# One 256-column accumulation in place of two of 128 for the sum of squares, with weights stored plain and doubled

## The chip, the core and the metric

The kernel runs on one core of one Trainium2 chip. Time is device microseconds (us) of that core, from launch to end; lower is better. The engines of the core are TensorE (PE; PEld is its weight load), VectorE (DVE), ScalarE (ACT), GpSimd (POOL) and SyncE (SP, which here only issues transfers). Each runs its own list of instructions in order, and they meet at semaphores.

## What is computed

A transformer block with adaptive layer norm on x of 4 x 1024 x 256: attention with 16 heads of 16, then a feed-forward part that picks one of 8 experts for each group of tokens by the smallest reconstruction loss. The part that matters here is the loss:

```python
h = relu(einsum('btd,ndh->bnth', x, W_enc) + b_enc)        # 8 experts, 64 hidden each
recon = einsum('nbth,nhd->nbtd', h, W_dec) + b_dec
losses = mean((recon - x) ** 2, axis=(2, 3))
top1 = argmin(losses, axis=0)
...
return base + adapter_out                                   # adapter of the chosen expert
```

The kernel doesn't form recon. The square of recon summed over the tokens is a sum over pairs of hidden units: (the sum over tokens of h_i h_j) times (W_dec W_dec^T)_ij. The first factor is a product of the hidden values with themselves on TensorE, the second is a table of weights, `ww`, computed once.

## The kernel before, in words

One list of steps, `S.list`, is worked out in Python by `order()`; every engine walks the same list and emits its part of each step, so the order on each engine is fixed when the program is built. A batch (b = 0 to 3) has 64 "units" of attention work: the E steps (scores, exponentiated by ACT into `P`), the PV steps (product with V into `pO`) and the M steps (scores whose row maximum DVE takes, line 1298). Between them `plan()` places the steps of the other stages: layer norm of the next batch (`ln1s` statistics on DVE, `ln1n` normalization on POOL at line 1662, `ln1turn` transposition on PE at line 907), `qk`, `v`, `proj`, and the feed-forward steps of the batch before (`enc`, `ehi`, `half`, `gsq`, `pick`, `select`, `fetch`, `mid`, `out`). After the last unit comes a tail, written out by hand, that ends with the second half of batch 3: `gsq` and `half`, `pick`, `select`, `fetch`, `mid`, `out`.

The banks of the PSUM are shared out in turn among all of these (`pM`, `pE`, `pX`; a step waits until the former user has emptied its bank).

The sum of squares is the step `gsq(b, i, th)`: batch b, pair i of the four groups of 128 hidden units, half th of the tokens, so 4 x 2 x 2 = 16 steps. The hidden values are held as two parts, high and low (`Hs[..., 0, :]` and `Hs[..., 1, :]`). For each group p PE multiplies the high part by both parts side by side, which leaves 256 columns in the bank: 128 of high times high, 128 of high times low. The second counts twice, since low times high is the same by symmetry. DVE then multiplies each 128 columns by `ww[:, p, :]` and adds them up (`tensor_tensor_reduce`, line 1491): with scale 1 for the first block and 2 for the second, into `acc[:, th, 1, p]` and `acc[:, th, 2, p]`. Each such reduction is two rows in a profile: the pass over the columns (CUSTOM_DVE_ANT_0) and the reading of the accumulator. It waits for the one before it (`link`), and the last of a step sets the bank free. The step `half(b, p, th)` does the same once over 258 columns with the table `wd` (line 1469). `pick` sums `acc` over its slots (line 1552).

The table is filled by the step `setupc` near the start (line 1633, DVE): 128 columns for each of 4 groups. `wsplit` (c = 0, 1) is a pair of steps on POOL that splits the encoder weights into high and low parts, `weh` and `wel` (lines 1750 and 1752); it becomes due at unit 24. The pair stands in POOL's list between the steps `ln1s(1, 1)` and `ln1n(1, 1)`.

SP issues all transfers in the order of the list: the moves of the operands `QO` and `KO` (line 1880), the maxima (`QO<-mT`, line 1938), the output of attention (`outs<-osb`, line 1891), the tiles of x for the next layer norm (`xin<-in_x`, line 1948), which wait for the transposition of the tile before. POOL issues 12 transfers of its own at the start (line 1700).

Of the kernel before, what the change touches and what calls it, by code (L numbers as in the profile page):

```python
# [11 lines left out]
ALU = mybir.AluOpType  # L12
# [537 lines left out]
def adaln_block(nc, x, wqkvT, wpT, pb, wbase, bbase, wenc, benc, bencc, wdec, wdecT, bdecT,  # L550
                wdown, bdown, wup, bup, cidx, cT, wmod, consts, out):
    ctx = ExitStack()
    with ctx:
        def sb(name, shape, dt=F):
            return ctx.enter_context(nc.sbuf_tensor(name, shape, dt))

        def sem(name):
            return ctx.enter_context(nc.semaphore(name))
# [34 lines left out]
        weh = sb("weh", [128, 2, 512], R)  # L593
        wel = sb("wel", [128, 2, 512], R)
        wd = sb("wd", [128, 4, D + 2])
        ww = sb("ww", [128, 4, 128])
        wdn = sb("wdn", [128, 2, H])
        wdh = sb("wdh", [128, 2, H], R)
        wdl = sb("wdl", [128, 2, H], R)
# [7 lines left out]
        modT2 = sb("modT2", [128, 4, NB])  # L607
        wdc = sb("wdc", [128, 4])
        sbc = sb("sbc", [128, 4])
# [13 lines left out]
        rec = sb("rec", [128, 4, 4])  # L623
        junk = sb("junk", [128, 258])
        junkx = sb("junkx", [128, 512])
        acc = sb("acc", [128, 2, 3, 4])
        ps = sb("ps", [128, 4])
        pl8 = sb("pl8", [128, 4, 2])
        pl8a = sb("pl8a", [128, 4, 2])
# [59 lines left out]
        s_Hh, s_Hl, s_HL, s_Xh, s_Xl = (sem(n) for n in ("Hh", "Hl", "HLd", "Xh", "Xl"))  # L689

        s_fill, s_rs1, s_xn, s_mhl, s_rs2, s_X = (sem(n) for n in ("fill", "rs1", "xn", "mhl", "rs2", "X"))
        s_modT2, s_sbc, s_wd = (sem(n) for n in ("modT2", "sbc", "wd"))

        s_hh, s_hl, s_hL, s_wen, s_wdn, s_wdL = (
            sem(n) for n in ("hh", "hl", "hL", "wen", "wdn", "wdL"))
# [16 lines left out]
        def bank(s):  # L712
            i = turn[s][0]
            return pM[:, i, :] if i < 3 else pE[:, i - 3, :] if i < 6 else pX[:, :]
# [6 lines left out]
        def full(*s):  # L721
            i, n = turn[s]
            return s_full[i], n + 1

        def emptied(*s):
            i, n = turn[s]
            return s_free[i], n + 1
# [4 lines left out]
        def empties(s):  # L732
            return s_free[turn[s][0]], 1
# [529 lines left out]
        def vector(e):  # L1263
            dve = Waits(e)
            link = Link(s_vlink)
# [22 lines left out]
            for s in S.list:  # L1288
                s, piece = step(s)
# [50 lines left out]
                elif kind == "be":  # L1340
# [4 lines left out]
                    for p in range(4):  # L1345
                        a = e.tensor_scalar(be[:, p, 2 * p:2 * p + 2], bmask, bec[:, p:p + 1], None, ALU.mult)
                    a.then_inc(s_be, 1)

                elif kind == "ln1s":
# [11 lines left out]
                    for t in range(2):  # L1361
                        a = e.bn_aggr(mv1[:, k, t, :], st1[:, k, t, :])
                    a.then_inc(s_mv1, 1)

                elif kind == "ln1n" and s[1] == 0:
# [3 lines left out]
                    for t in range(2):  # L1369
                        a = e.tensor_scalar(xt[:, t, :], xt[:, t, :], mv1[:, k, t, 0:1], rs1[:, k, 1, t:t + 1],  # L1370
                                            ALU.subtract, ALU.mult)
# [25 lines left out]
                elif kind == "ln2s":  # L1397
                    b, k = s[1:]
                    dve.wait_ge(*link.now())
                    for t in (2 * k, 2 * k + 1):  # L1400
                        a = e.bn_aggr(mv2[:, t, :], st2[:, t, :])
                    a.then_inc(s_mv2, 1)

                elif kind == "ln2n" and s[1] == LAST:
# [6 lines left out]
                    for t in (2 * k, 2 * k + 1):  # L1411
                        a = e.tensor_scalar(Xr[:, t % 4, :], x2[:, t, :], mv2[:, t, 0:1], rs2[:, 1, t:t + 1],
                                            ALU.subtract, ALU.mult)
# [50 lines left out]
                elif kind == "half" and last:  # L1464
                    b, p, th = s[1:]
# [7 lines left out]
                elif kind == "gsq":  # L1473
                    b, i, th = s[1:]
                    if (b, i, th) == (LAST, 0, 1):
# [5 lines left out]
                        e.tensor_tensor(pl8a[:, :, :], ps[:, :].unsqueeze(2).to_broadcast([128, 4, 2]),  # L1481
                                        bmask.unsqueeze(1).to_broadcast([128, 4, 2]), ALU.mult).then_inc(s_pick, 1)
                        dve.wait_ge(s_pick, 2 * b + 2)
                    dve.wait_ge(*full("setupc"))
                    dve.wait_ge(*full(*s))
                    for p in (2 * i, 2 * i + 1):

                        for r in range(2):
                            dve.wait_ge(*link.now())
                            n = 256 * (p % 2) + 128 * r  # L1490
                            a = e.tensor_tensor_reduce(junk[:, 0:128], bank(s)[:, n:n + 128], ww[:, p, :], r + 1.0, 0.0,
                                                       ALU.mult, ALU.add, acc[:, th, 1 + r, p:p + 1])
                            a.then_inc(*(empties(s) if p % 2 and r else link.up()))
                    dve.wait_ge(*emptied(*s))

                elif kind == "xhi" and alone(s[1], s[2] // 2):
# [141 lines left out]
        def gpsimd(e):  # L1638
# [8 lines left out]
            for s in S.list:  # L1647
# [98 lines left out]

                elif kind == "wsplit":
                    c = s[1]
                    pool.wait_ge(d_w[6], 16)
                    e.tensor_copy(weh[:, c, :], wenc_s[:, c, :]).then_inc(*link.up())  # L1750
                    pool.wait_ge(*link.now())
# [288 lines left out]
```

## Time and profile before

| | us |
|---|---|
| median of 3 runs | 980.05 |
| lowest and highest of them | 978.15, 981.6 |
| the profiled execution, its own time | 980.53 |
| span of the profile, from first to last instruction | 978.7 |
| busy: PE, DVE, ACT, POOL | 945.7, 793.5, 657.7, 335.8 |
| granted TensorE clock, mean | 0.983 |

The span is 1.8 us less than the profiled execution's own time (980.53 - 978.7); that part lies outside the instructions. Busy time is the union of an engine's rows. PE is busy for 97% of the span, DVE for 81%; TensorE's clock is granted at 0.98 of its full 2.4 GHz on the mean. Where a row says "[0.32 <-POOL xin L1662]", the engine stood idle for 0.32 us before it, and the write of `xin` on POOL at line 1662 ended that wait.

### The profile page before, as it was taken

What the parts mean: (1) busy time and instruction counts of PE and PEld (TensorE: products, weight loads), DVE (VectorE), ACT (ScalarE), POOL (GpSimd) and SP (SyncE); (2) the same over time, 40 slices, a digit from 0 to 9 for tenths busy, and PEclk for the clock granted to TensorE, in tenths of its full rate; (3) what the DMA queues carried; (4) which work ended last, traced back from release to release, by engine and by line L of the source; (5) the groups of instructions that cost most, each with busy time, mean ns of one, the idle gap of its engine ahead of it and who ended that gap; (6) DMA issues with size and microseconds to landing.
All of it is one profiled execution on the core that took longest, in us unless ns stands there. A gap on an engine that the chain in (4) does not pass through costs nothing.

```text
span 978.7 us, 16476 instructions
## 1 busy us (share of the span) xinstructions
PE 945.7 (97%) x5794; PEld 475.7 (49%) x5794; DVE 793.5 (81%) x1629; ACT 657.7 (67%) x1295; POOL 335.8 (34%) x447
## 2 busy tenths in 40 slices
PE   6999999989999999999999999999999999999998
PEld 4444344434344355544454455445445465644486
DVE  4789988978888787887788888778878888888365
ACT  2148887877786777666668786766657867566930
POOL 4050234124364343111456543410165613116320
PEclk9889999999999899999999999999999999999999
DMA  6932061342525311416342411405434321132001
GB/s 180 144 73 39 23 110 46 61 93 73 94 49 89 60 36 35 77 27 110 99 105 50 87 35 46 75 14 88 127 82 83 52 36 36 39 98 79 30 6 49
DMA packets 47890, 66.93 MB, mean 68 GB/s; under 512 B 12139, under 2 KB 32112, under 8 KB 47796
## 3 DMA queue, kind: packets, MB, share of 16 engines
q1 hardware_dynamic: 46572, 65.00, 31.4%
q0 software_dynamic: 384, 0.79, 0.6%
q8 instruction: 46, 0.75, 0.4%
q14 instruction: 36, 0.29, 0.1%
q10 hardware_dynamic: 852, 0.09, 0.1%
HBM read 27.48 MB, written 12.59 MB: 41 GB/s over the span
## 4 chain that ended last, share of the span: by engine, by line
PE 75%; DVE 10%; DMA 5%; SPq 4%; ACT 2%; issue 2%; POOL 2%; ACTq 0%; DVEq 0%; POOLq 0%
PE pE L813 23%; PE pM L813 22%; PE pO L813 20%; PE pX L813 8%; DVE mx L1298 7%; SPq L1880 2%; DMA QO<-lo 1%; DMA xin<-in_x 1%; DMA QO<-mT 1%; ACT P L1120 1%; DMA outs<-osb 1%; PE pM L907 1%; ACT h1T L1161 1%; DVE junk L1435 1%; SPq L1938 1%
## 5 line engine op out<-in xcount | busy, mean ns | idle before, releaser
L1298 DVE TENSOR_REDUCE mx<-pE 128x1 f32<-128x512 f32 x440 | 287.2, 683 | 48.7 <-PE pE L813 47.4
L1298 DVE TENSOR_REDUCE mx<-pM 128x1 f32<-128x512 f32 x447 | 294.4, 683 | 31.2 <-PE pM L813 29.6
L1120 ACT ACTIVATE P<-pM 128x512 f32<-128x512 f32 x457 | 260.9, 602 | 69.2 <-PE pM L813 67.7
L1120 ACT ACTIVATE P<-pE 128x512 f32<-128x512 f32 x431 | 243.3, 602 | 86.9 <-PE pE L813 85.8
L813 PE MATMUL pO<-P,V 128*17 128x512 f32 x2048 | 261.7, 607 | 1.2 <-ACT osb L1127 1.0
L813 PE MATMUL pM<-KO,QO 48*128 48x512 f32 x447 | 178.7, 446 | 4.1 <-DMA QO<-lo 3.6
L813 PE MATMUL pM<-QO,KO 50*128 50x512 f32 x457 | 178.6, 435 | 1.0
L813 PE MATMUL pE<-KO,QO 48*128 48x512 f32 x440 | 175.0, 447 | 3.3 <-DVE mx L1298 2.5
L813 PE MATMUL pE<-QO,KO 50*128 50x512 f32 x431 | 166.2, 437 | 3.5 <-DMA QO<-mT 3.0
L813 PEld LDWEIGHTS pM<-QO,KO 50*128 50x128 f32 x457 | 80.8, 187 | 101.4 <-issue 70.8
L813 PEld LDWEIGHTS pE<-QO,KO 50*128 50x128 f32 x431 | 76.0, 187 | 99.4 <-issue 75.7
L1298 DVE TENSOR_REDUCE mx<-pX 128x1 f32<-128x512 f32 x137 | 93.7, 684 | 16.9 <-PE pX L813 16.2
L1120 ACT ACTIVATE P<-pX 128x512 f32<-128x512 f32 x136 | 81.3, 598 | 21.8 <-PE pX L813 21.4
L813 PEld LDWEIGHTS pO<-P,V 128*17 128x17 f32 x2048 | 40.9, 96 | 102.1 <-issue 92.2
L813 PEld LDWEIGHTS pM<-KO,QO 48*128 48x128 f32 x447 | 78.3, 188 | 17.1 <-issue 6.8
L813 PEld LDWEIGHTS pE<-KO,QO 48*128 48x128 f32 x440 | 75.9, 187 | 16.3 <-DVE mx L1298 7.0
L1706 POOL CAST mh<-mxc 128x16 fp32r<-128x16 f32 x32 | 6.3, 198 | 175.5 <-DVE mxc L1307 175.4
L813 PE MATMUL pX<-KO,QO 48*128 48x512 f32 x137 | 62.0, 453 | 2.5 <-DMA QO<-lo 1.1
L813 PE MATMUL pX<-QO,KO 50*128 50x512 f32 x136 | 58.9, 433 | 1.3 <-DVE mx L1298 1.1
L1765 POOL TENSOR_TENSOR Hs<-h2f,Hs 128x512 fp32r<-128x512 f32 x28 | 35.7, 1282 | 67.1 <-ACT Hs L1240 52.9
L1692 POOL CAST hi<-lo 128x512 fp32r<-128x512 f32 x28 | 17.3, 619 | 73.6 <-ACT lo L1180 73.6
L813 PEld LDWEIGHTS pX<-QO,KO 50*128 50x128 f32 x136 | 25.6, 188 | 26.9 <-issue 18.5
(303 smaller groups left out, 1323.0 us busy)
## 6 DMA issues: line engine op xcount, KB each, us to landing
outs<-osb SPq DMA_DIRECT2D x31, 256.0 KB, 2.2
KO<-hi SPq DMA_DIRECT2D x56, 128.0 KB, 4.0
QO<-hi SPq DMA_DIRECT2D x56, 128.0 KB, 5.6
x<-in_x SPq DMA_DIRECT2D x20, 256.0 KB, 3.5
out<-x SPq DMA_DIRECT2D x16, 256.0 KB, 2.1
AT<-outs SPq DMA_DIRECT2D x15, 256.0 KB
asum<-wsum SPq DMA_DIRECT2D x15, 256.0 KB
KO<-lo SPq DMA_DIRECT2D x28, 128.0 KB, 3.7
```

What stands on the lines that cost most here:

```text
L813: return e.matmul(o, lhsT, rhs, start=start, stop=stop)
L907: a = e.transpose(o[:, 256 * c + 128 * t:256 * c + 128 * t + 128], tokens(b, k)[:, t, 128 * c:128 * c + 128], ident)
L1120: e.activation(P[:, u % 3, j, :], bank(s), ACT.Exp).then_inc(*empties(s))
L1161: a = e.activation(h1T[:, c, 256 * k:256 * k + 256], bank(s)[:, 256 * c:256 * c + 256], ACT.Identity, bias=modT[:, c, b:b + 1], scale=modT ...
L1298: e.tensor_reduce(mx[:, hq % 2, k:k + 1, kh], bank(s), AX.X, ALU.max, negate=True).then_inc(*empties(s))
L1435: e.tensor_tensor_reduce(junk[:, 0:D], wd[:, p, 0:D], bc[:, 1, :], 1.0, 0.0, ALU.mult, ALU.add, sbc[:, p:p + 1]).then_inc(*link.up())
L1692: e.tensor_copy(hi[:, cs], lo[:, cs].bitcast(F)).then_inc(s_qh, 1)
L1706: e.tensor_copy(mh[:, :], mxc[:, :]).then_inc(*link.up())
L1765: e.tensor_tensor(Hs[:, t % 4, :, 1, :], h2f[:, t % 2, :].rearrange("p (a n) -> p a n", a=4), Hs[:, t % 4, :, 0, :].bitcast(F), ALU.subtra ...
L1880: e.dma_start(*move(gi, w, i, thirds(gi, w))).then_inc(landed(gi)[0], 16)
L1938: e.dma_start(*rows(hq, j)).then_inc(d_m[hq % 2][j], 16)
```

## The change

`ww` gets 256 columns for each group: the plain weights in columns 0 to 127 as before, and twice the weights in columns 128 to 255. DVE makes one reduction over the 256 columns of a group, with scale 1, where it made two over 128. `acc` loses one of its three slots. The doubled half is written by POOL, in the second `wsplit` step, from the plain half, and `gsq` waits for that (`s_ww`) in place of `setupc`. The memory set aside for the descriptors of POOL's own transfers goes from 4096 to 2048 bytes per partition, which makes room for the larger table.

```diff
-        ww = sb("ww", [128, 4, 128])
+        ww = sb("ww", [128, 4, 256])
...
-        acc = sb("acc", [128, 2, 3, 4])
+        acc = sb("acc", [128, 2, 2, 4])
...
-                    dve.wait_ge(*full("setupc"))
+                    dve.wait_ge(s_ww, 1)
                     dve.wait_ge(*full(*s))
                     for p in (2 * i, 2 * i + 1):
 
-                        for r in range(2):
-                            dve.wait_ge(*link.now())
-                            n = 256 * (p % 2) + 128 * r
-                            a = e.tensor_tensor_reduce(junk[:, 0:128], bank(s)[:, n:n + 128], ww[:, p, :], r + 1.0, 0.0,
-                                                       ALU.mult, ALU.add, acc[:, th, 1 + r, p:p + 1])
-                            a.then_inc(*(empties(s) if p % 2 and r else link.up()))
+                        dve.wait_ge(*link.now())
+                        n = 256 * (p % 2)
+                        a = e.tensor_tensor_reduce(junk[:, 0:256], bank(s)[:, n:n + 256], ww[:, p, :], 1.0, 0.0,
+                                                   ALU.mult, ALU.add, acc[:, th, 1, p:p + 1])
+                        a.then_inc(*(empties(s) if p % 2 else link.up()))
...
                 elif kind == "wsplit":
                     c = s[1]
+                    if c:
+                        pool.wait_ge(*emptied("setupc"))
+                        e.tensor_scalar(ww[:, :, 128:256], ww[:, :, 0:128], 2.0, None, ALU.mult).then_inc(s_ww, 1)
                     pool.wait_ge(d_w[6], 16)
...
-    nc = bacc.Bacc("TRN2", target_bir_lowering=False, num_devices=1, dynamic_dma_scratch_size=4096)
+    nc = bacc.Bacc("TRN2", target_bir_lowering=False, num_devices=1, dynamic_dma_scratch_size=2048)
```

The order on PE, ACT and SP is the same in both kernels. On POOL one instruction is added. POOL before, from the second statistics of the next layer norm to the third (`rs` is the inverse deviation, `xin` the tile that PE transposes, `mh` and `mhl` the maxima in two parts):

```order
L1655 TENSOR_TENSOR rs<-rs,nh 128x2
L1750 CAST weh<-h2f 128x512
L1752 TENSOR_TENSOR wel<-h2f,weh 128x512
L1750 CAST weh<-h2f 128x512
L1752 TENSOR_TENSOR wel<-h2f,weh 128x512
L1662 TENSOR_SCALAR xin<-xin,mv,rs 128x256 x2
L1706 CAST mh<-mxc 128x16
```

The same place on POOL now:

```order
L1654 TENSOR_TENSOR rs<-rs,nh 128x2
L1752 CAST weh<-h2f 128x512
L1754 TENSOR_TENSOR wel<-h2f,weh 128x512
L1750 TENSOR_SCALAR ww<-ww 128x4x128
L1752 CAST weh<-h2f 128x512
L1754 TENSOR_TENSOR wel<-h2f,weh 128x512
L1661 TENSOR_SCALAR xin<-xin,mv,rs 128x256 x2
L1705 CAST mh<-mxc 128x16
```

The doubling stands between the two halves of the weight split, ahead of the normalization of `xin` and of the first conversion of the maxima.

On DVE the reductions of a `gsq` step go from four to two. DVE before in the tail, the last of the two `gsq` steps of the last half batch, then the last `half` and the first two rows of `pick`:

```order
L1491 ISA junk,acc<-pM,ww 128x128
L1491 ISA acc 128x1
L1491 ISA junk,acc<-pM,ww 128x128
L1491 ISA acc 128x1
L1491 ISA junk,acc<-pM,ww 128x128
L1491 ISA acc 128x1
L1491 ISA junk,acc<-pM,ww 128x128
L1491 ISA acc 128x1
L1469 ISA junk,acc<-pE,wd 128x258
L1469 ISA acc 128x1
L1552 TENSOR_REDUCE ps<-acc 128x4
L1554 TENSOR_TENSOR pl<-ps,cst 128x8
```

The same place on DVE now:

```order
L1490 ISA junk,acc<-pM,ww 128x256
L1490 ISA acc 128x1
L1490 ISA junk,acc<-pM,ww 128x256
L1490 ISA acc 128x1
L1469 ISA junk,acc<-pE,wd 128x258
L1469 ISA acc 128x1
L1551 TENSOR_REDUCE ps<-acc 128x4
L1553 TENSOR_TENSOR pl<-ps,cst 128x8
```

Nothing else changes place; two pairs of rows are gone from every `gsq` step, and the remaining ones are twice as wide.

## Rows read from the trace of the kernel before

**Rows 1.** The page: busy time of each engine, its share, instructions.

```profile
PE 945.7 (97%) x5794; PEld 475.7 (49%) x5794; DVE 793.5 (81%) x1629; ACT 657.7 (67%) x1295; POOL 335.8 (34%) x447
```

**Rows 2.** The page: the chain that ended last, by engine.

```profile
PE 75%; DVE 10%; DMA 5%; SPq 4%; ACT 2%; issue 2%; POOL 2%; ACTq 0%; DVEq 0%; POOLq 0%
```

**Rows 3.** Instructions of line 1491 and who waited for them; ns minimum/median/maximum.

```profile
L1491 DVE CUSTOM_DVE_ANT_0 junk<-pE,ww x32: 281/291/294, 406.9 to 950.4; 128x128 f32<-128x128 f32 x32
...
  PEld pX L813: 1.5, 2
  PE pX L813: 0.7, 1
  PEld pE L813: 0.5, 1
```

**Rows 4.** Instructions of line 1469, the reduction over 258 columns.

```profile
L1469 DVE CUSTOM_DVE_ANT_0 junk<-pM,wd x11: 417/427/428, 351.0 to 944.8; 128x258 f32<-128x258 f32 x11
```

**Rows 5.** Timeline of DVE near the end: start us, us, engine, line, instruction.

```profile
944.34 0.43 DVE L1469 CUSTOM_DVE_ANT_0 junk<-pX,wd 128x258 f32<-128x258 f32 x1
...
944.81 0.43 DVE L1469 CUSTOM_DVE_ANT_0 junk<-pM,wd 128x258 f32<-128x258 f32 x1
...
948.04 0.28 DVE L1491 CUSTOM_DVE_ANT_0 junk<-pE,ww 128x128 f32<-128x128 f32 x1
...
950.70 0.69 DVE L1459 TENSOR_TENSOR h2f<-pX,nbe 128x512 f32<-128x512 f32 x1
```

**Rows 6.** Timeline of PE, 649 to 650 us.

```profile
649.63 0.50 PE L813 MATMUL pX<-KO,QO 48*128 48x512 f32 x1 [0.70 <-DVE acc L1491]
```

**Rows 7.** Timeline, the two other places where PE waits for line 1491.

```profile
344.98 0.18 PEld L813 LDWEIGHTS pX<-KO,QO 48*128 48x128 f32 x1 [0.49 <-DVE acc L1491]
...
572.83 0.18 PEld L813 LDWEIGHTS pE<-KO,QO 48*128 48x128 f32 x1 [0.50 <-DVE acc L1491]
...
573.90 0.34 PEld L813 LDWEIGHTS pO<-P,V 128*17 128x17 f32 x8 [0.51 <-ACT P L1120]
```

**Rows 8.** Timeline of PE and PEld in the tail, weight loads and products of the last `half`.

```profile
956.32 0.42 PEld L813 LDWEIGHTS pE<-Xs,Hs 128*128 128x128 f32 x3 [0.23 <-DVE Hs L1533]
956.92 1.14 PEld L813 LDWEIGHTS pE<-Xs,Hs 128*128 128x128 f32 x9 [0.18 <-DVE Hs L1533]
...
960.73 1.62 PE L813 MATMUL pE<-Xs,Hs 128*128 128x258 f32 x12
```

**Rows 9.** Timeline of DVE in the tail, the last `half`, right behind `gsq`.

```profile
962.76 0.43 DVE L1469 CUSTOM_DVE_ANT_0 junk<-pE,wd 128x258 f32<-128x258 f32 x1
```

**Rows 10.** Timeline of POOL in and after the second half of the weight split.

```profile
133.58 0.62 POOL L1750 CAST weh<-h2f 128x512 fp32r<-128x512 f32 x1
134.27 1.28 POOL L1752 TENSOR_TENSOR wel<-h2f,weh 128x512 fp32r<-128x512 f32 x1
135.53 2.45 POOL L1662 TENSOR_SCALAR xin<-xin,mv,rs 128x256 f32<-128x256 f32 x2
137.93 0.20 POOL L1706 CAST mh<-mxc 128x16 fp32r<-128x16 f32 x1
```

**Rows 11.** Timeline of PE, the transposition that reads `xin`.

```profile
138.13 0.63 PE L907 MATMUL pE<-cst,xin 128*128 128x128 f32 x4 [0.32 <-POOL xin L1662]
```

**Rows 12.** Groups of POOL: busy us, mean ns of one, idle before.

```profile
L1789 POOL TENSOR_SCALAR rs<-mv 128x2 f32<-128x2 f32 x16 | 3.7, 234 | 22.2 <-DVE mv L1401 22.2
L1811 POOL TENSOR_SCALAR bc<-bc 128x256 f32<-128x256 f32 x4 | 3.4, 862 | 15.7 <-DVE wd L1445 15.7
```

**Rows 13.** Timeline of SP and DVE after that place.

```profile
141.74 0.45 SPq L1948 DMA_DIRECT2D xin<-in_x  x1
...
146.18 0.75 DVE L1359 BATCH_NORM_STATS2 st<-xin 128x6 f32<-128x256 f32 x2 [0.38 <-DMA xin<-in_x]
```

**Rows 14.** Pieces of the chain that ended last, two landings of `QO<-lo`: start, us, what.

```profile
21.02 5.29 DMA QO<-lo
...
250.86 9.16 DMA QO<-lo
```

More of the change, by code:

```diff
@@ L691, in adaln_block @@
         s_fill, s_rs1, s_xn, s_mhl, s_rs2, s_X = (sem(n) for n in ("fill", "rs1", "xn", "mhl", "rs2", "X"))
-        s_modT2, s_sbc, s_wd = (sem(n) for n in ("modT2", "sbc", "wd"))
+        s_modT2, s_sbc, s_wd, s_ww = (sem(n) for n in ("modT2", "sbc", "wd", "ww"))
         s_hh, s_hl, s_hL, s_wen, s_wdn, s_wdL = (
```

## The prediction

> **What bounds the kernel now.** I read the busy shares first, then the chain of work that ended last, then the timeline around each instruction that the change touches. PE is busy for 97% of the span and DVE for 81% [rows 1]; the chain lies 75% on PE and 10% on DVE [rows 2]. So time taken off DVE is worth something only where PE is waiting for DVE, and a delay is worth its full length wherever PE waits for the delayed thing. Busy totals can't decide this change; sixteen `gsq` steps and one spot on POOL can.
>
> Around the 64 reductions of line 1491 the list of those who waited is short: 1.5, 0.7 and 0.5 us in four entries, of which two describe the same wait, once for the weight load and once for the product [rows 3]. It is three places, at 345, 573 and 650 us. In the tail the chain is serial and DVE has its turn twice.
>
> **The change on DVE.** A 128-column pass takes 291 ns [rows 3], and the read of the accumulator comes behind it. The cost of both in a row is the distance of the starts: eight of them fill the time from 948.04 to 950.70, so 2.66 / 8 = 0.333 us each. The new shape doesn't occur, but its neighbour does: 258 columns, one operand in the PSUM and one table in SBUF, 427 ns [rows 4], with 944.81 - 944.34 = 0.47 us from start to start [rows 5]. So a pair costs 2 x 0.333 = 0.67 us before and 0.47 after, 0.195 us less; a step (two pairs) 0.39 us less; all 32 pairs 6.2 us less of DVE's time. That is 0.6% of the span, and an upper bound of the gain.
>
> **What of it reaches the path, in the loop.** Twelve of the sixteen steps lie among the attention units; 12 x 0.39 = 4.7 us is their bound. At 650 us PE waits 0.70 us for the last reduction of a step [rows 6]; that step ends 0.39 earlier, and the step before it hands on about 0.1 more, since DVE doesn't rest between the two: 0.5 us gained. At 345 us the weight load waits 0.49 us; about 0.17 of this is the usual gap between two loads, so 0.3 is left. At 573 us there is the same wait of 0.50, but half a microsecond behind it PE waits 0.51 for ACT, whose work doesn't hang on this step [rows 7]; what is gained is lost there: 0. At the other nine steps DVE comes to rest, or is held by PE, before PE needs it; I give them 0.1 together. Sum 0.9 us; bounds 0.2 (only half of the place at 650) and 4.7 (every step on the path).
>
> **What reaches it in the tail.** The first eight reductions (948.04 to 950.70, [rows 5]) stand ahead of the chain `enc`, `ehi`, `elo` that feeds `half`. They shrink by 0.78 us, and PE's two waits for `Hs`, 0.23 and 0.18 us [rows 8], nearly vanish: PE runs 0.38 us earlier. The last eight shrink by 0.78 too. Before, the last `half` reduction starts on DVE at 962.76, right behind `gsq` [rows 9], while the product that it reads ends at 960.73 + 1.62 = 962.35 [rows 8]. After, `gsq` would be done by 961.6, and the product, 0.38 earlier, ends at 961.97; the reduction starts at about 962.05, 0.7 us earlier. Between it and the last product of `select` PE has small products of its own to do, which moved by only 0.38; so I take 0.6. Everything behind (`select`, `fetch`, `mid`, `out`) hangs on that product and moves with it. Bounds 0.38 and 0.78.
>
> **The change on POOL.** One tensor_scalar of 128 x 512 is added. POOL has no such shape. Of one-operation tensor_scalars it has 2 columns in 234 ns and 256 in 862 ns [rows 12]: 2.47 ns per column, so 512 cost 0.862 + 256 x 0.00247 = 1.5 us. Bounds: 0.6 us, as the conversion of the same size, and 2.46 us, two of the two-operation ones over 256 columns, which take 2.45 [rows 10].
>
> The price of the place is the point. POOL is 34% busy over the span [rows 1], but not here: from 133.58 to 138.1 us its rows follow each other without a gap, conversion, subtraction, normalization of `xin`, maxima [rows 10]. The doubling goes ahead of all of them. The normalization ends at 135.53 + 2.45 = 137.98 and PE's transposition, next in PE's list, starts at 138.13 after a wait of 0.32 us for it [rows 11]. There is no cover at all: PE is already waiting, so the transposition starts 1.5 us later, and the rest of PE's list with it. The maxima (`mh`) are late by as much too, but PE's transposition of them stands behind several more bursts of scores, so they cost nothing. The wait for `setupc` costs nothing either: DVE does that step near the start, far ahead of this place.
>
> Some is given back. The next tile's transfer is issued at 141.74, held by other transfers and not by the transposition, and DVE waits 0.38 us for it at 146.18 [rows 13]. With PE and DVE 1.5 us late the tile is there in time, so 0.38 is absorbed. Further waits for transfers up to 343 us hang on moves released by PE's or DVE's own progress and shift along. Net cost 1.5 - 0.38 = 1.1 us; bounds 0.2 and 2.1.
>
> Here a page bears on the size. The row says 2.47 ns per column, some 3 cycles of a 1.2 GHz engine. The Trainium skill, page "GPSIMD Engine Reference", section 3.1 "Elementwise — side-by-side cycle accounting", says that a loop body of up to two operations goes at 1.03 cycles per element, limited by the port alone. By that 512 elements would take, as an estimate, 0.44 us and the dispatch; no row of a POOL tensor_scalar here is that fast.
>
> The smaller `acc` shortens two tiny sums on DVE by 4 to 8 elements: nothing. The smaller descriptor memory touches only the 12 transfers that POOL issues at the start.
>
> **The sum.** -0.9 (loop) - 0.6 (tail) + 1.1 (POOL) = -0.4 us. Against the profiled execution, 980.53, that is 980.1. That execution is 0.5 above the median of the runs, 980.05, so the forecast for a median is 979.7. A difference under 0.3%, 2.9 us, is about what a measurement of this kernel can't tell from no change.
>
> **Rivals.**
> *All of the gain reaches the path.* Moving DVE forward may let PE run ahead at steps where I see no wait, since each relieved bank also feeds the next burst of scores. For it: DVE is on the chain for 10% [rows 2]. Against it: only three waits name line 1491 [rows 3]. It gives -4.7 - 0.6 + 1.1 = -4.2, so 975.9. Half of it would give 977.9. Chance of being faster by over 2.9: 0.13.
> *The doubling is cheap.* It costs 0.6 us like the conversion [rows 10]; net cost 0.6 - 0.38 = 0.2, sum -1.3, so 978.8. It is the result of the page's rule, and still within 0.3%. Chance 0.12.
> *The doubling is dear.* 2.46 us, 2.1 net, and only 0.2 gained in the loop: +1.3, so 981.3. This one is slower than before, and decides from the point where the doubling costs more than 0.38 + 0.9 + 0.6 = 1.9 us; still within 0.3%. Chance 0.12.
> *A late transfer.* The stall at 138 us moves all of PE's later requests against transfers that are already under way. The same move `QO<-lo` took 5.29 us at one place of the chain and 9.16 at another [rows 14]. One more meeting of this kind costs 9.16 - 5.29 = 3.9 us: -0.4 + 3.9 = +3.5, so 983.6. For it: DMA is 5% of the chain [rows 2]. Against it: PE shifts by only 1.1 us. Chance 0.07.
> *The halved descriptor memory holds POOL up.* Its 12 early transfers would wait for each other, with operands for the first scores behind them. One such landing, at the 5.29 us of the early `QO<-lo` [rows 14], would make +4.9, so 985. Chance 0.04.
> *The wide pass isn't cheaper.* If it took the 0.67 us of two, the gain is zero and the cost stays: +1.1, so 981.2. Against it stand 32 rows of 258 columns at 427 ns [rows 4]. Chance 0.02.
>
> **How the numbers follow.** The forecast, two small effects that nearly cancel, has the other 0.50. The likeliest time is 979.7. Faster by over 0.3%: 0.13. Slower by over 0.3%: 0.07 + 0.04 = 0.11, and 0.01 for the dear doubling together with something else: 0.12. Within: 0.75. The range reaches from the middle of the first rival, with some 0.08 below it, to beyond the dear doubling, with some 0.09 above it: 977.0 to 982.6.
>
> **What would show it.** In the changed profile: line 1490 with 32 passes at 420 to 428 ns and 32 reads; the doubling on POOL at about 133.6 us with 1.5 us; the wait of the transposition for `xin` at 1.8 us in place of 0.32, and the 0.38 us wait of DVE for the next tile gone; the rows up to 131 us unchanged in time; PE at 345 us about 1.1 us later than before; the 0.70 us wait at 650 down to about 0.2; and the last `half` reduction 0.6 to 0.7 us nearer to the end of the preceding `gsq`'s product than now. The prediction is wrong if the shift after 140 us isn't about 1.1 us, or if the distance from 345 us to the tail shrinks by much more than 0.9.

## The result

The changed kernel takes 983.0 us (median of 22 runs, 980.25 to 990.02) against 979.93 us for the kernel before (22 runs beside them, 978.05 to 985.83). The ratio is 1.0034, 95% interval 1.0019 to 1.0049: slower by 0.34%, some 3.1 us. The forecast was 979.7, within 0.3%, with a range up to 982.6. The time lies 0.4 us above the range, and the sign of the difference is not the one forecast.

Nearly every single term of the sum came out as predicted. One term was missing: what the pause before the transposition does to TensorE's clock.

The page after, busy time and chain by engine, which answer to [rows 1, 2]:

```profile
PE 948.2 (97%) x5794; PEld 477.6 (49%) x5794; DVE 787.9 (80%) x1565; ACT 656.9 (67%) x1295; POOL 336.7 (34%) x448
...
PE 78%; DVE 9%; DMA 4%; ACT 3%; SPq 2%; issue 2%; POOL 2%; ACTq 0%; DVEq 0%
```

PE has the same 5794 products and is busy 2.5 us longer (945.7 before). The same work takes longer: this is the first sign that it isn't only a matter of waiting. The profiled execution took 982.64 us, its span is 980.8 (978.7 before) and its mean granted clock 0.979 (0.983 before).

**The reductions.** Line 1490 in the profile after (count, ns minimum/median/maximum, first and last start), and who waited for it (us, times), which answer to [rows 3]:

```profile
L1490 DVE DVE_READ_ACCUMULATOR2_ANT acc<- x32: 81/83/85, 348.8 to 964.1; 128x1 f32 x32
L1490 DVE CUSTOM_DVE_ANT_0 junk<-pE,ww x16: 413/424/427, 411.3 to 952.3; 128x256 f32<-128x256 f32 x16
...
  PEld pX L813: 0.8, 2
  PE pX L813: 0.3, 1
```

A wide pass takes 424 ns. The timeline of DVE in the tail (start us, us, instruction) gives the distance of the starts, and the rows answer to [rows 5, 9]:

```profile
950.91 0.42 DVE L1490 CUSTOM_DVE_ANT_0 junk<-pE,ww 128x256 f32<-128x256 f32 x1
...
952.30 0.42 DVE L1490 CUSTOM_DVE_ANT_0 junk<-pE,ww 128x256 f32<-128x256 f32 x1
...
952.77 0.69 DVE L1459 TENSOR_TENSOR h2f<-pX,nbe 128x512 f32<-128x512 f32 x1
...
964.78 0.43 DVE L1469 CUSTOM_DVE_ANT_0 junk<-pE,wd 128x258 f32<-128x258 f32 x1 [0.55 <-PE pE L813]
```

Four fill 952.77 - 950.91 = 1.86 us, 0.465 each. The last `half` reduction now waits for its product by 0.55 us, where it stood right behind `gsq` before. At 650 us the wait of 0.70 [rows 6] has become 0.30:

```profile
651.73 0.49 PE L813 MATMUL pX<-KO,QO 48*128 48x512 f32 x1 [0.30 <-DVE acc L1490]
```

**The doubling.** The timeline of POOL, PE and DVE after, which answers to [rows 10, 11, 13]:

```profile
133.06 1.52 POOL L1750 TENSOR_SCALAR ww<-ww 128x512 f32<-128x512 f32 x1
...
136.50 2.45 POOL L1661 TENSOR_SCALAR xin<-xin,mv,rs 128x256 f32<-128x256 f32 x2
```

```profile
139.09 0.63 PE L907 MATMUL pE<-cst,xin 128*128 128x128 f32 x4 [1.83 <-POOL xin L1661]
...
141.26 2.00 PE L813 MATMUL pE<-wqkv_s,h1T 128*128 128x256 f32 x4
143.19 0.79 PE L813 MATMUL pE<-QO,KO 50*128 50x512 f32 x1
```

```profile
148.12 0.74 DVE L1359 BATCH_NORM_STATS2 st<-xin 128x6 f32<-128x256 f32 x2
```

It takes 1.52 us, and PE's wait has grown from 0.32 to 1.83, by 1.51. DVE no longer waits for the next tile. All that was predicted. What wasn't stands in the last row of PE: a product of 512 columns takes 0.79 us, where it takes 0.50 at 139.65 in the same profile. Stretches of 4 us show why (columns: stretch, us; busy us and count of PE, PEld, DVE, ACT, POOL; granted clock; share of DMA; GB/s). After:

```profile
137.00:141.00 4.00, 1.95 (x14) 1.07 (x10) 1.58 (x5) 1.58 (x4) 2.48 (x5) 1.00 0.59 102
141.00:145.00 4.00, 4.00 (x15) 2.07 (x19) 2.06 (x4) 2.82 (x7) 0.00 (x0) 0.57 0.47 117
145.00:149.00 4.00, 4.00 (x33) 1.41 (x29) 3.85 (x10) 3.00 (x8) 0.00 (x0) 1.00 0.09 25
...
202.00:206.00 4.00, 3.89 (x16) 1.35 (x18) 1.89 (x3) 1.93 (x4) 0.00 (x0) 0.60 0.20 24
206.00:210.00 4.00, 4.00 (x12) 1.65 (x12) 1.89 (x4) 1.97 (x5) 0.00 (x0) 0.50 0.56 171
210.00:214.00 4.00, 4.00 (x22) 1.03 (x24) 2.54 (x5) 2.23 (x5) 0.00 (x0) 0.62 0.71 225
```

The same stretches before:

```profile
141.00:145.00 4.00, 4.00 (x30) 1.26 (x29) 3.22 (x7) 3.56 (x8) 0.00 (x0) 1.00 0.43 115
...
202.00:206.00 4.00, 4.00 (x18) 1.16 (x10) 2.29 (x4) 2.48 (x5) 0.00 (x0) 0.66 0.19 67
206.00:210.00 4.00, 4.00 (x31) 1.50 (x32) 3.65 (x7) 3.15 (x6) 0.00 (x0) 1.00 0.73 191
210.00:214.00 4.00, 4.00 (x22) 1.60 (x22) 3.82 (x8) 3.15 (x6) 0.58 (x3) 1.00 0.41 141
```

Behind the longer pause PE's clock is granted at half, 1.2 in place of 2.4 GHz, for most of the stretch from 141 to 145 us (0.57 on the mean), and PE does 15 products where it did 30. It is busy throughout, so that nothing in busy shares or waits names the loss. The half clock doesn't begin with the first product behind the pause: the transposition starts at 139.09, and the clock falls at 141.4. Near 200 us PE waits for `QO<-mT` in both kernels, before and after:

```profile
200.17 0.47 PE L813 MATMUL pE<-QO,KO 50*128 50x512 f32 x1 [2.68 <-DMA QO<-mT]
```

```profile
202.11 0.46 PE L813 MATMUL pE<-QO,KO 50*128 50x512 f32 x1 [2.71 <-DMA QO<-mT]
```

The half clock behind that lasts from 201.3 to 204.7 before, and from 202.8 to 213.0 in this profile of after.

**Where the time went in this pair of profiles.** I took the start of the same product on PE in both, and the difference (after minus before):

| place, us | difference | step | what lies there |
|---|---|---|---|
| 137 | -0.54 | -0.54 | differences of the first 137 us |
| 139 | +0.97 | +1.51 | the longer wait for `xin` |
| 143 | +2.50 | +1.53 | half clock behind it |
| 150 | +1.93 | -0.57 | wait for the next tile absorbed |
| 212 | +4.91 | +2.98 | longer half clock after the wait for `QO<-mT` |
| 340 | +4.71 | -0.20 | |
| 346 | +4.41 | -0.30 | `gsq` at 345 |
| 470 | +4.43 | +0.02 | |
| 490 | +2.64 | -1.79 | a half-clock stretch at 481 in before's profile alone |
| 580 | +2.45 | -0.19 | `gsq` at 573 |
| 655 | +2.10 | -0.35 | `gsq` at 650, less than 0.1 of it drift |
| 880 | +1.93 | -0.17 | |
| 940 | +2.87 | +0.94 | a half-clock stretch at 885 in after's profile alone |
| 974 | +2.13 | -0.74 | the tail |

The stretches at 481 and 885 stand in one profile each and behind no change of the order: further profiles, below, have such stretches at 715, 904, 909 or 912 or nowhere. Which of the entries belong to the change, one pair can't tell. That is what the experiments are for.

### The profile page after: what moved, and what is told of

Same layout as the page of the kernel before. It is cut to its first block, busy times and chain, and to the rows that moved or that the text cites. A ratio compares the mean times of both kernels' runs of the same rounds, so it can differ in the third digit from the quotient of the medians.

```text
span 980.8 us, 16414 instructions
## 1 busy us (share of the span) xinstructions
PE 948.2 (97%) x5794; PEld 477.6 (49%) x5794; DVE 787.9 (80%) x1565; ACT 656.9 (67%) x1295; POOL 336.7 (34%) x448
## 4 chain that ended last, share of the span: by engine, by line
PE 78%; DVE 9%; DMA 4%; ACT 3%; SPq 2%; issue 2%; POOL 2%; ACTq 0%; DVEq 0%
PE pE L813 24%; PE pM L813 23%; PE pO L813 21%; PE pX L813 9%; DVE mx L1298 6%; SPq L1882 2%; DMA QO<-lo 1%; ACT P L1120 1%; DMA QO<-mT 1%; ACT h1T L1161 1%; DVE junk L1435 1%; DMA xin<-in_x 1%; PE pM L907 1%; DMA P<-in_wmod 0%; DVE st L1395 0%
## 5 line engine op out<-in xcount | busy, mean ns | idle before, releaser
L813 PE MATMUL pM<-QO,KO 50*128 50x512 f32 x457 | 180.6, 439 | 0.9
```

What stands on the lines that cost most here:

```text
L813: return e.matmul(o, lhsT, rhs, start=start, stop=stop)
```

## The experiments

The theory: the doubling's place costs its length and, behind it, a stretch of half clock on PE that the longer pause brings on; without the half clock the change would be as forecast, about nothing. The rivals: the layout or the halved descriptor memory costs the time; the new order on DVE does; the rest is chance.

Times are compared with runs of the kernel before on the same chip in the same rounds. Their median is 980.97 us beside the doubling near the start, the doubling alone, the layout alone and the four products; 982.0 beside the two products, the doubling behind `xin`, the doubling twice, and the doubling near the start with the pause at 200 us filled; 980.76 beside the last three, the changed kernel once more and it and the kernel before with that pause filled. Times of different groups are compared by their ratios to before. The ratios are those on record, with 95% intervals; they differ from the quotient of the two medians by up to 0.14%.

### The doubling near the start

The changed kernel, but POOL doubles the table right behind DVE's `setupc`, near the start, in place of the second `wsplit`.

```diff
+                elif kind == "setupc":
+                    pool.wait_ge(*emptied(*s))
+                    e.tensor_scalar(ww[:, :, 128:256], ww[:, :, 0:128], 2.0, None, ALU.mult).then_inc(s_ww, 1)
...
                 elif kind == "wsplit":
                     c = s[1]
-                    if c:
-                        pool.wait_ge(*emptied("setupc"))
-                        e.tensor_scalar(ww[:, :, 128:256], ww[:, :, 0:128], 2.0, None, ALU.mult).then_inc(s_ww, 1)
```

> The changed kernel, but POOL doubles the table in the step setupc near the start, where POOL stands idle for 25 us, instead of between the halves of the weight split. Theory A (the loss is PE's pause for xin at 138 us and the half clock that follows it): no pause and no half-clock stretch at 141 us; what is left is the gain of the wide reductions, -0.3 at 345, -0.2 at 573, -0.4 at 650 and -0.75 in the tail, so about -1.5 us, 978.4. Rival B (the loss comes from the wide reductions, the smaller descriptor memory or the moved tables): it stays slower than before by 2 us or more.

Measured: 978.91 us, ratio 0.9973 (0.9953 to 0.9994). One of the 12 executions took 4684 us and is left out of the ratio; the median of the other 11 is 978.71. The kernel is faster than before by 0.27%, and so some 0.6% faster than the changed kernel, by the place of one instruction of 1.5 us. PE's transposition and the products behind it, and the stretch that follows:

```profile
138.66 0.63 PE L907 MATMUL pE<-cst,xin 128*128 128x128 f32 x4 [0.31 <-POOL xin L1661]
...
140.82 1.13 PE L813 MATMUL pE<-wqkv_s,h1T 128*128 128x256 f32 x4
```

```profile
141.00:145.00 4.00, 4.00 (x28) 1.74 (x32) 3.22 (x7) 3.58 (x8) 0.00 (x0) 1.00 0.34 82
```

The wait is 0.31 again, the clock full, and the four products of `wqkv_s` take 1.13 us in place of 2.00. The gains of the wide reductions stay: -0.29 at 345, -0.19 at 573, -0.42 at 650, -0.80 in the tail. What DVE gains is worth its 1.7 us (their sum) once the doubling is out of the way. The wide reductions on DVE are acquitted.

### The doubling alone

The kernel before with narrow reductions, plus the doubling at the changed kernel's place, into a table that nobody reads, and the smaller descriptor memory.

```diff
+        ww2 = sb("ww2", [128, 4, 128])
...
                     c = s[1]
+                    if c:
+                        pool.wait_ge(*emptied("setupc"))
+                        e.tensor_scalar(ww2[:, :, :], ww[:, :, :], 2.0, None, ALU.mult)
...
-    ... dynamic_dma_scratch_size=4096)
+    ... dynamic_dma_scratch_size=2048)
```

> The kernel before with its narrow reductions; a spare table in SBUF, the smaller descriptor memory, and the same doubling on POOL in the second wsplit step, written to the spare table that nobody reads. Theory A: PE pauses 1.5 us longer at 139 us, a stretch at half clock follows and costs about 1.5 more, some 0.5 is absorbed: +2.5 us at least, and more than the changed kernel by the 1.5 us that its reductions save, so +3 to +5. A theory of the pause alone, without the clock: +1.0. Rival B: nothing, within 0.5 us.

Measured: 983.61 us, ratio 1.0021 (0.9997 to 1.0045). The interval just holds 1, so by time alone this is weak; the profile is not:

```profile
139.12 0.63 PE L908 MATMUL pE<-cst,xin 128*128 128x128 f32 x4 [1.82 <-POOL xin L1663]
...
141.28 2.08 PE L814 MATMUL pE<-wqkv_s,h1T 128*128 128x256 f32 x4
```

```profile
141.00:145.00 4.00, 4.00 (x15) 2.17 (x19) 1.98 (x4) 2.75 (x6) 0.00 (x0) 0.57 0.57 134
```

The wait, the half clock, and the shift of PE against before (-0.51 at 137, +0.99 at 139, +2.55 at 143, +1.97 at 150) are those of the changed kernel's first profile within 0.05 us, without a single wide reduction. At 345, 573 and 650 this kernel gains nothing (0.01 each), and in the tail nothing either (+0.01). The time alone doesn't show what was expected further, that this kernel is slower than the changed one by the gain of its reductions: 1.0021 here, 1.0034 there, with intervals wider than that gain.

### The layout alone

The kernel before with the same spare table, never written, and the descriptor memory of 2048 bytes.

```diff
+        ww2 = sb("ww2", [128, 4, 128])
...
-    ... dynamic_dma_scratch_size=4096)
+    ... dynamic_dma_scratch_size=2048)
```

> The kernel before with the smaller descriptor memory and a spare table in SBUF, so that the tensors lie where the changed kernel has them; no instruction differs. Theory A: no difference, within 0.5 us. Rival B in its form of the descriptor memory: slower by 2 us or more.

Measured: 980.59 us, ratio 0.9991 (0.9966 to 1.0017). PE stands where it stood before, within 0.2 us, from 100 to 470 us. Memory and layout are out as a cause.

### PE kept busy in the pause

The changed kernel, and ahead of the transposition's wait PE makes products that nobody uses, the identity by 512 columns of `wqkv_s`, into the bank that the transposition then overwrites. Four of them:

```diff
                     b, k = s[1:]
+                    if (b, k) == (1, 1):
+                        for _ in range(4):
+                            mm(o, ident, wqkv_s[:, 0, 0:512])
                     pe.wait_ge(s_xn if b else s_xn0, nth["ln1n", b, k] - (4 if b else 0))
```

> The changed kernel; ahead of the wait for xin of ln1turn(1, 1) PE makes four products of the identity with 512 columns of wqkv_s into the bank that the transposition overwrites. They fill the pause of 1.8 us, the doubling stays where it is. Theory A: the pause keeps its length but the stretch at half clock after it is gone, so 1.5 us or more faster than the changed kernel, at +1 to +1.5 over before. A theory of the pause alone: no faster than the changed kernel, +3.

Measured: 980.91 us, ratio 1.0004 (0.9985 to 1.0023). Each of these products is two instructions of 0.46 us, so that the four took 3.7 us, twice the pause: PE was 3.91 us late at 139 (with 0.78 at 137) against 0.97 in the changed kernel. Yet the clock stayed full from 141 to 145, and although 2 us had been thrown away, the kernel was no slower than before, and better than the 1 to 1.5 us of loss expected. Behind the wait at 200 us (2.73 here) the half clock lasts from 205.7 to 212.6, twice as long as before, although there was none at 141; PE's shift grows there by 1.4:

```profile
141.00:145.00 4.00, 3.78 (x17) 2.04 (x15) 1.84 (x3) 2.30 (x5) 0.00 (x0) 1.00 0.41 92
...
206.00:210.00 4.00, 4.00 (x14) 1.74 (x12) 1.92 (x4) 2.17 (x4) 0.00 (x0) 0.50 0.45 151
```

The edit was mis-sized; the next one puts it right, with two products:

```diff
-                        for _ in range(4):
+                        for _ in range(2):
```

> As the run that filled the pause, but with two products of the identity with 512 columns in place of four: each turned out to be two instructions of 0.46 us, so four took 3.7 us and held PE 2 us longer than the doubling does; two take 1.85 us, the length of the pause. Theory A (the pause costs 1.5 us, the half clock behind it 1.5 more): clock 1.00 from 141 to 145 us, PE 1.5 to 1.7 us late at 143 us and not 3.0 as in the changed kernel, the whole 1 to 1.5 us faster than the changed kernel, near 981. A theory of the pause alone: PE 3.0 us late at 143 us whatever PE does in the pause.

```profile
137.47 1.98 PE L813 MATMUL pE<-wqkv_s,cst 128*128 128x512 f32 x4
139.29 0.65 PE L910 MATMUL pE<-cst,xin 128*128 128x128 f32 x4
```

```profile
141.00:145.00 4.00, 3.95 (x25) 1.97 (x25) 3.22 (x7) 3.57 (x8) 0.00 (x0) 1.00 0.52 128
```

Measured: 981.5 us, ratio 0.9999 (0.9981 to 1.0017). The transposition starts as late as in the changed kernel (the shift grows by 1.45 there, from -0.27 to 1.18), so the delay is all there, but the clock is 1.00 and the shift goes to 1.17 at 143 and 0.70 at 150. **This is the run that tells most.** With the delay kept and the half clock gone, the change is worth what the prediction said of it, nothing that can be measured (-0.04% forecast, -0.01% measured, interval -0.19 to +0.17%). The delay itself was priced rightly.

### The doubling behind xin

The changed kernel, with the doubling on POOL right behind the normalization of `xin`, ahead of the maxima.

```diff
+                    if (b, k) == (1, 1):
+                        pool.wait_ge(*emptied("setupc"))
+                        e.tensor_scalar(ww[:, :, 128:256], ww[:, :, 0:128], 2.0, None, ALU.mult).then_inc(s_ww, 1)
...
                     c = s[1]
-                    if c:
-                        pool.wait_ge(*emptied("setupc"))
-                        e.tensor_scalar(ww[:, :, 128:256], ww[:, :, 0:128], 2.0, None, ALU.mult).then_inc(s_ww, 1)
```

> The changed kernel, with the doubling on POOL one step later: behind the normalization of xin, ahead of the maxima. Theory A (only what PE waits for costs, and at this place it waits for xin alone): no pause at 138 us, no half clock at 141, as fast as with the doubling near the start, -1.5 to -2.7 us against before. Rival (the place costs because POOL is dense there, whoever is behind it): the maxima are 1.5 us late, PE or SP waits for them, and it is slower than with the doubling near the start by 1 us or more.

```profile
138.27 0.63 PE L907 MATMUL pE<-cst,xin 128*128 128x128 f32 x4 [0.31 <-POOL xin L1661]
```

Measured: 979.68 us, ratio 0.9981 (0.9961 to 1.0001). PE waits 0.31 us for `xin`, the clock stays full, and the shift is 0.15 at 137 and 0.13 at 143. It is 0.59 at 150, as DVE waits 0.83 us for the next tile; with the doubling near the start that wait is 0.72 and the shift grows alike, by 0.35. The maxima are 1.5 us late here and nobody on PE is: the prediction's claim that they have cover holds. So it is the place ahead of `xin` by one instruction of POOL that costs, not the doubling.

### The doubling twice

The doubling alone once more, but done twice, so that the pause is longer by 1.5 us again.

```diff
                         pool.wait_ge(*emptied("setupc"))
+                        e.tensor_scalar(ww2[:, :, :], ww[:, :, :], 2.0, None, ALU.mult).then_inc(*link.up())
+                        pool.wait_ge(*link.now())
                         e.tensor_scalar(ww2[:, :, :], ww[:, :, :], 2.0, None, ALU.mult)
```

> The kernel before with the doubling into a spare table made twice, one behind the other, in the second wsplit step: 3.0 us on POOL. Theory A: PE's pause grows by 3.0 us and the half clock follows once, so PE is 3.0 + 1.5 to 2 us late at 145 us, and the whole is +4.5 to +6 us. If the clock loss grew with the pause, it would be +3.0 in its place and the whole +7 or more. A theory of the pause alone: +2.5.

```profile
140.48 0.63 PE L908 MATMUL pE<-cst,xin 128*128 128x128 f32 x4 [3.37 <-POOL xin L1663]
```

```profile
141.00:145.00 4.00, 4.00 (x13) 2.25 (x12) 1.94 (x3) 2.48 (x5) 0.00 (x0) 0.52 0.52 133
145.00:149.00 4.00, 4.00 (x21) 1.41 (x20) 2.36 (x5) 2.43 (x5) 0.00 (x0) 0.62 0.04 9
```

Measured: 984.85 us, ratio 1.0040 (1.0023 to 1.0057), some 3.9 us, a little under the 4.5 to 6 expected. The shift goes from -0.70 at 137 to 2.35 where the transposition starts (the pause, 3.05) and 4.97 when the half clock is over: it lasts into the next stretch, from 141.2 to 148.0, and costs 2.62 us, where it cost 1.56 in the profile of the single doubling. And the long half clock at 203 us is not there: in this profile it takes 3.4 us as in before, and PE's shift goes from 4.40 at 150 to 4.41 at 212. So that one isn't a fixed consequence of a late PE.

### The changed kernel once more

To see which stretches return, the changed kernel with no edit.

> The changed kernel as it is, on the chip and in the rounds of the next two runs. It should be +2 to +4 us against before, with the same pause at 138 us and the clock at 0.57 from 141 to 145 us. What is asked of it: whether the long stretch at half clock behind the second pause (202.8 to 213 us, in this kernel and in the one with the doubling alone; 3.4 us long in before) comes again.

```profile
140.27 0.83 PE L907 MATMUL pE<-cst,xin 128*128 128x128 f32 x4 [1.83 <-POOL xin L1661]
```

```profile
141.00:145.00 4.00, 4.00 (x13) 2.34 (x12) 1.89 (x3) 2.48 (x5) 0.00 (x0) 0.50 0.39 102
145.00:149.00 4.00, 4.00 (x25) 1.55 (x28) 2.66 (x5) 2.73 (x6) 0.00 (x0) 0.70 0.15 40
...
206.00:210.00 4.00, 4.00 (x16) 1.12 (x8) 2.28 (x5) 2.54 (x5) 0.00 (x0) 0.65 0.19 67
210.00:214.00 4.00, 4.00 (x31) 1.47 (x30) 3.65 (x7) 3.11 (x6) 0.00 (x0) 1.00 0.67 179
```

Measured: 983.02 us, ratio 1.0032 (1.0013 to 1.0051), the same as the first time. The wait of 1.83 us and the half clock behind it come back, this time from 140.6 to 147.4 us: the half clock begins earlier, in the transposition itself (0.83 us in place of 0.63). The shift goes from 0.63 at 137 to 2.15 where the transposition starts (1.52, the pause) and 4.66 when the half clock is over, so that this costs 2.51 us for the same pause that cost 1.53 the first time, and nearly as much as behind the pause of twice the added length. The long one at 203 does not come back (+0.0 from 150 to 212). The half clock behind the doubling's pause is thus in every profile of a kernel that leaves this pause open, and lasts 3.4 us in two of them and 6.8 in three (the third, below, is the changed kernel with another pause filled); that near 200 is common to all that leave that pause open, and its length varies too.

### Filling the pause at 200 us

Every kernel above waits 2.4 to 2.7 us for `QO<-mT` at 200 us and then runs at half clock. Three of the same unused products stand ahead of that wait, 2.8 us, in three kernels: the one with the doubling near the start, the changed one, and the one before.

```diff
                     gi, c = SEQ[hq]
+                    if (u, j) == (48, 0):
+                        for _ in range(3):
+                            mm(o, ident, wqkv_s[:, 0, 0:512])
                     if gi:
                         pe.wait_ge(*landed(gi))
```

With the doubling near the start:

> The kernel with the doubling near the start; in addition PE makes three products of the identity with 512 columns of wqkv_s, 2.8 us, into its own free bank while it waits 2.6 us for QO<-mT at 198 to 201 us (unit 48). Theory A, carried to another pause: the stretch at half clock that now follows at 202 us is gone, which gives 1.0 to 1.7 us, so 977.2 to 977.9. If that stretch isn't due to the pause: no gain, within 0.5 us of the kernel with the doubling near the start.

```profile
198.82 2.84 PE L813 MATMUL pE<-wqkv_s,cst 128*128 128x512 f32 x6
```

```profile
202.00:206.00 4.00, 4.00 (x26) 1.44 (x23) 3.63 (x6) 3.64 (x7) 0.00 (x0) 1.00 0.20 65
```

Measured: 976.11 us, ratio 0.9954 (0.9936 to 0.9972). The clock stays full where it was 0.66 before, and the shift goes from +1.34 at 200.5 us to -0.25 at 212: 1.6 us gained by work that nobody needs. A second half-clock stretch, at 238 us, went too, for reasons that I didn't find. The time is 1.1 us below the 977.2 to 977.9 expected; the shift shows the second stretch to be worth 1.45. The kernel leaves nothing of the computation out, and it is faster than both kernels of this document.

In the changed kernel:

> The changed kernel with the three products in the second pause, at unit 48, and nothing in the first. If the 2.8 us that the changed kernel loses between 201 and 213 us are the clock behind the second pause, they go, and the stretch of before with them: PE between 200 and 213 us gains 3.5 to 4 us on the changed kernel, the whole is 3 to 4 us faster than it, about 979. If the first pause is what makes the second stretch long, and filling the second can't help, it gains 1 us at most.

```profile
141.00:145.00 4.00, 4.00 (x12) 2.38 (x12) 1.89 (x3) 2.57 (x6) 0.00 (x0) 0.50 0.30 76
...
202.00:206.00 4.00, 4.00 (x19) 1.32 (x17) 1.43 (x3) 1.41 (x3) 0.00 (x0) 1.00 0.63 88
```

Measured: 980.3 us, ratio 0.9998 (0.9981 to 1.0015). The pause at 138 is left as it is, with its half clock (0.50 from 141 to 145). At 200 the shift falls from 3.74 to 2.15, again 1.6, and at 238 by 1.45 more. The changed kernel with one pause filled is level with the kernel before.

In the kernel before:

> The kernel before, with narrow reductions, and the same three products in its second pause. It parts the gain of the fill from that of the wide reductions: the stretch at 201 us goes, -1.0 to -1.7 us; the kernel with early doubling and fill stays ahead of it by the 1.5 us of the reductions.

```profile
202.00:206.00 4.00, 4.00 (x24) 1.60 (x23) 3.62 (x6) 3.51 (x7) 0.00 (x0) 1.00 0.22 71
```

Measured: 978.8 us, ratio 0.9973 (0.9959 to 0.9987). The shift goes from 1.04 to -0.43 over the pause, 1.5 gained; the stretch at 237 stayed here. The profile has one more half-clock stretch, at 715 us, that costs it 3.2 us and that no other profile has; the median of the runs is faster than before all the same.

### The clock over all runs

Each run records a mean granted clock. Over the runs of each kernel it is:

| kernel | runs | mean clock | time, us | PE's added pause at 138 |
|---|---|---|---|---|
| before | 88 | 0.9822 | 980 to 982 | none |
| changed | 22 | 0.9784 | 983.0 | 1.51 |
| changed, once more | 12 | 0.9792 | 983.02 | 1.51 |
| doubling alone | 12 | 0.9800 | 983.61 | 1.50 |
| doubling twice | 8 | 0.9797 | 984.85 | 3.05 |
| changed, pause filled (two) | 12 | 0.9826 | 981.5 | filled |
| changed, pause filled (four) | 12 | 0.9842 | 980.91 | filled |
| doubling behind `xin` | 12 | 0.9819 | 979.68 | none |
| doubling near the start | 11 | 0.9840 | 978.91 | none |
| layout alone | 12 | 0.9831 | 980.59 | none |
| changed, 200 filled | 12 | 0.9823 | 980.3 | 1.5 |
| before, 200 filled | 10 | 0.9860 | 978.8 | none |
| near the start, 200 filled | 7 | 0.9880 | 976.11 | none |

The four kernels with the open pause at 138 and nothing filled lie at 0.978 to 0.980, all others at 0.982 or above; to fill 200 lifts each kernel by 0.003 to 0.004. Among the runs of one kernel, time goes with clock: the correlation is -0.95 over the 22 runs of the changed kernel and -0.96 over the 88 of before, with 7.7 and 8.8 us less for 0.01 of clock more. The changed kernel's mean clock is 0.0038 lower than before's; by these slopes that is 2.9 to 3.4 us, about the whole measured difference of 3.1. The runs of before in this table are those of the experiments, since those beside the 22 runs have no clock on record; but the changed kernel once more, at 0.9792, stands beside runs of before at 0.9829 in the same rounds, 0.0036 apart, which says the same. This is a comparison of means and an estimate, but it agrees with the filled pause: take the clock out, and what is left of the change is near zero.

## Why the prediction was wrong

Point by point, by its own steps:

| step | predicted | measured |
|---|---|---|
| a wide pass, start to start | 0.47 us | 0.465 |
| gain at 345, 573, 650, elsewhere in the loop | 0.3, 0, 0.5, 0.1 | 0.30, 0.19, 0.35 to 0.42, little |
| loop, sum | 0.9 | 0.9 |
| tail | 0.6 | 0.74 (0.80 near the start) |
| doubling | 1.5 us | 1.52 |
| added wait on PE | 1.5 | 1.51 |
| absorbed at the next tile | 0.38 | 0.57 |
| maxima late | 0 | 0 |
| layout, descriptor memory | 0 | -0.09%, interval holds 0 |
| clock behind the pause | not in the sum | +1.5 to +2.5 |

The sum in these terms is -0.9 - 0.74 + 1.51 - 0.57 = -0.7, for -0.4 predicted. On that the prediction was right. It was wrong at 573, where I gave nothing because PE waited for ACT half a microsecond behind; 0.19 came through. This is small.

**The step that failed is "The price of the place".** It said "the transposition starts 1.5 us later, and the rest of PE's list with it" and took the pause for a delay that moves everything behind it and changes nothing else. But the work behind a pause of 1.8 us isn't done at the pace of the work ahead of it. Behind the old pause of 0.32 us PE's clock stayed full; behind 1.83 it was granted at half, after 2.3 us in the first profile and 0.3 in the second, and 15 products were done in the 4 us that had held 30. This cost 1.53 us more in the first profile, 2.51 in the second, and 2.62 behind the pause of 3.37. The profile before had shown it all: at 200 us PE waits 2.7 us for `QO<-mT`, and the 4 us behind have 18 products at 0.66. I read there what ends the wait, not what follows it.

The Trainium skill has a rule of this kind, page "TensorE: Matmul & The Clock Gate", Part 1, in "HAM oscillation — how this bites in real kernels": a wait for data makes the engine cold again, so that the work that follows starts at the lower clock. The page tells it of waits longer than the one here, so it doesn't foresee this case by itself; the trace goes further than the page: 1.83 us of wait, then 0.57, and 2.68 before, then 0.66. With a price taken from that, the forecast would have had one rival more: -0.4 and the price at the pause near 200 us, 4 us at 0.66, so 4 x 0.34 = 1.4 us lost: +1.0, or 981.1. It would have moved the centre and the chances, though it alone doesn't reach 983.0.

**What stays open.** By the places, the change costs -0.7 + 1.5 to 2.5 = +0.8 to +1.8 us, and the measured difference is +3.1 with an interval from 1.9 to 4.8. So 0.1 us at least, and 1.8 us by the middle values, is not accounted for by what every profile of it shows. The long half clock at 203 us (3.0 us more) was in the first profile of the changed kernel and in that of the doubling alone, not in the second of the changed one nor with the doubling twice; behind the four products, where PE was 3.4 us late at 200 with its clock full at 141, a shorter form of it cost 1.4. Such a stretch in half of the executions would make 1.5 us on the mean and nearly close the account; two or three profiles of five are no proof. The mean clock allows it: 0.0038 less over 980 us is, as an estimate, 980 x 0.0038 / 0.5 = 7.4 us more at half clock in each execution, and the stretch at 141 us is 3.4 or 6.8 of them.

Nor does the length of a pause alone tell what follows: in the profile before, PE waits 1.11 us at 236 us and 1.57 at 323, and is at half clock from 238.9 to 242.3 and from 324.2 to 331.0, but it waits 1.14 at 259 and the clock stays full. What sets whether such a stretch comes and how long it is, and why filling the pause at 200 took the stretch at 238 away in two kernels and not in the third, wasn't settled.

The rival *the doubling is cheap* is refuted: it had 0.6 us from the conversion of the same size, and the doubling takes 1.52. The estimate of 0.44 us that the prediction worked out from the Trainium skill's page "GPSIMD Engine Reference", section 3.1, isn't borne out by that row either. The rivals *a late transfer* and *the halved descriptor memory* gave times near the measured one, 983.6 and 985, for reasons that are not the cause: the wait for the transfer at 200 us is 2.71 us against 2.68, and the layout alone costs nothing.

## What to carry to other kernels

Where PE waits already, a delay can cost its length and then a stretch of half clock, some 1.5 to 2.6 us here for pauses of 1.8 to 3.4, and not in proportion to them; so look, in the profile before, at the granted clock behind the pauses that are already there and add that price. Small work for another engine belongs where its in-order list has cover: the same 1.5 us instruction made the kernel 0.3% slower ahead of `xin`, and left it 0.3% faster near the start. Where a pause of PE can't be avoided, a few products that nobody uses, no longer than the pause, can be worth as much as the optimization under study (-0.27% for filling the pause at 200 in the kernel before, -0.27% for the change with its doubling near the start, -0.46% for both).

## What the runs showed of the hardware

A busy TensorE can be a slow one. In the stretch from 206 to 210 us of the changed kernel PE is busy 4.00 of 4.00 us and does 12 products, and 31 in the same stretch before; the busy share is the same, and the columns of the count and of the granted clock (0.50 and 1.00) tell the two apart.

A product of 512 columns in 32-bit floats, with the identity as its other factor, is two instructions of 0.46 us at full clock (the row of 2.84 us for six, 0.47 each), which is why the first filling was twice too long.

On POOL a one-operation tensor_scalar takes 862 ns for 256 columns [rows 12] and 1516 for 512: 2.55 ns for each further column, and a fixed part near 0.2 us.
